# Dispatch scatters moved to other expert tiles, and a new row order for the result buffer, in an attention and mixture-of-experts kernel

## The reference

```
bids = sigmoid(einsum('bsh,eh->bse', x, conf_w) + conf_b) * wealth
top_bids, selected_experts = top_k(bids, 2)
routing_weights = softmax(top_bids, axis=-1)
expert_out = silu(x @ gate_w[e]) * (x @ up_w[e]) @ down_w[e]
x = x + sum over the two experts of routing_weight * expert_out
```

## Time and profile before

| | |
|---|---|
| median of three executions | 403.84 us |
| profiled execution | 400.13 us |
| its span, first to last instruction | 398.4 us |
| TensorE busy | 313.8 us (79%) |
| VectorE busy | 277.0 us (70%) |
| ScalarE busy | 231.0 us (58%) |
| GpSimd busy | 219.3 us (55%) |
| mean granted TensorE clock | 0.901 of full |

### The profile page before, as it was taken

How to read it: one execution, slowest core, us unless ns; L and a number is a source line. 1 busy time by engine, 2 the same in 40 slices (tenths; PEclk the granted TensorE clock), 3 DMA queues, 4 the chain that set the end, 5 groups by cost and what they waited for, 6 DMA issues and landing times.

```text
span 398.4 us, 12299 instructions
## 1 busy us (share of the span) xinstructions
PE 313.8 (79%) x4430; PEld 255.4 (64%) x4430; DVE 277.0 (70%) x770; ACT 231.0 (58%) x464; POOL 219.3 (55%) x301
## 2 busy tenths in 40 slices
PE   6797989869797977767878886779899999988400
PEld 5575756547574755557657775568788888877400
DVE  5799998797988989894745754467556556635355
ACT  4786867584775859604656834346566566646300
POOL 6202065785858688784785586545545555654300
PEclk9899988998889899865989998699999999999955
DMA  7221404114050310111322222353575574221099
GB/s 267 92 95 43 133 2 157 32 20 157 14 169 22 112 38 16 35 35 42 61 63 61 48 61 69 113 83 112 170 204 151 149 214 141 48 56 36 6 302 330
DMA packets 47722, 39.45 MB, mean 99 GB/s; under 512 B 32550, under 2 KB 39084, under 8 KB 47664
## 3 DMA queue, kind: packets, MB, share of 16 engines
q1 hardware_dynamic: 43344, 30.20, 26.5%
q0 software_dynamic: 4320, 8.47, 7.0%
HBM read 15.16 MB, written 12.21 MB: 69 GB/s over the span
## 4 chain that ended last, share of the span: by engine, by line
PE 40%; DVE 26%; ACT 11%; issue 8%; another core or an unknown queue 7%; DMA 5%; SPq 2%; DVEq 0%; ACTq 0%; POOLq 0%
PE scores L1204 6%; DVE Pm L884 5%; PE bank L1366 4%; PE bank L1364 4%; PE bank L1365 3%; PE bank L1345 3%; PE bank L1347 3%; ACT hid_hi L777 3%; DVE Kexp L1117 2%; PE bank L1346 2%; DVE Vexp L856 2%; DMA w_hi<-by_token 2%; PE scores L1347 2%; PE scores L1345 2%
## 5 line engine op out<-in xcount | busy, mean ns | idle before, releaser
L601 POOL DMA_INDIRECT by_token<-y_sb,row_meta x71 | 79.8, 1124 | 73.1 <-ACT y_sb L761 58.2
L528 POOL DMA_INDIRECT by_expert<-token_rows,rows_to x64 | 69.2, 1081 | 31.5 <-issue 17.7
L1117 DVE TENSOR_TENSOR Kexp<-hid,hid_hi 128x512 f16<-128x512 f32 x71 | 49.1, 693 | 50.4 <-ACT hid_hi L777 47.9
L1111 DVE SCALAR_TENSOR_TENSOR hid<-scores,silu 128x512 f32<-128x512 f32 x71 | 47.4, 686 | 24.2 <-remote 8.0
L1204 PE MATMUL scores<-qT,Kexp 32*128 32x128 f32 (+1 forms) x1024 | 44.0, 315 | 16.3 <-DVE Pm L884 13.7
L1204 PEld LDWEIGHTS scores<-qT,Kexp 32*128 32x128 f32 x1024 | 39.1, 221 | 26.0 <-DVE Pm L884 20.8
L777 ACT ACTIVATE hid_hi<-hid 128x512 f16<-128x512 f32 x71 | 44.6, 628 | 19.0 <-DVE hid L1111 10.5
L1364 PE MATMUL bank<-w_hi,hid_hi 128*128 x248 | 45.3, 223 | 9.3 <-DVE Kexp L1117 7.3
L770 ACT ACTIVATE silu<-bank 128x512 f32<-128x512 f32 x71 | 40.5, 597 | 20.1 <-remote 8.7
L1365 PE MATMUL bank<-w_lo,hid_hi 128*128 x248 | 44.5, 222 | 2.5 <-issue 2.4
L884 DVE TENSOR_TENSOR Pm<-scores,causal 128x512 f32<-128x512 f32 x64 | 41.1, 684 | 6.4 <-ACT Pm L683 5.3
(11 more groups left out here) (291 smaller groups left out, 741.2 us busy)
## 6 DMA issues: line engine op xcount, KB each, us to landing
w_raw<-in_w_pack_dram SPq DMA_DIRECT2D x8, 768.0 KB, 4.6
x_all<-in_x_tok_dram SPq DMA_DIRECT2D x8, 256.0 KB, 5.1
cT<-in_ctx_t_dram SPq DMA_DIRECT2D x8, 256.0 KB, 4.5
w_hi<-by_token SPq DMA_DIRECT2D x4, 512.0 KB, 7.4
w_lo<-by_token SPq DMA_DIRECT2D x4, 512.0 KB, 8.0
out_dram<-x_all SPq DMA_DIRECT2D x8, 256.0 KB, 6.3
by_expert<-pad_row SPq DMA_DIRECT2D x9, 130.0 KB
by_token<-y_sb,row_meta POOLq DMA_INDIRECT x71
```

Source lines behind the costliest of these rows:

```text
L528: pool.indirect_dma_start(by_expert, bass.IndirectOffsetOnAxis(ap=rows_to[u % 2][:, s, b:b + 1], axis=0), token_rows[u % 2][:, b, s, :], N ...
L601: pool.indirect_dma_start(by_token, bass.IndirectOffsetOnAxis(ap=row_number[:, i % METAS, s, 1:2], axis=0), y_sb[:, k, s, :], None, bounds ...
L1117: dve.tensor_tensor(hid_lo[:, k % 2, slot, :], hid[:, slot, :], hid_hi[:, k % 2, slot, :], ALU.subtract).then_inc(lo_done, 1)
```

## The change

The diff has three parts. The row order in `by_token` goes from (unit, sequence, token, choice) to (unit, token, sequence, choice): `pair_id` is made with other strides, and the view `back` that the final loads read is the matching one, so that the eight results of one partition and unit lie in 4 KB in a row. Of unit 6, piece 0 stays ahead of `tail(7)`, piece 1 comes after it, and pieces 2 and 3 follow the result scatters of tiles 0 and 1. Of unit 7, the four pieces follow the result scatters of tiles 6, 8, 9 and 11.

```diff
-            back = by_token.rearrange("(u b t s) d -> u t b s d", u=UNITS, b=UB, s=TOP)
+            back = by_token.rearrange("(u t b s) d -> u t b s d", u=UNITS, b=UB, s=TOP)
...
-            made(pool.iota(pair_id[:], [[TOP * L, UB], [1, TOP]], base=0, channel_multiplier=TOP))
+            made(pool.iota(pair_id[:], [[TOP, UB], [1, TOP]], base=0, channel_multiplier=TOP * UB))
...
             tail_rows(UNITS - 2, (UNITS - 2) % 2)
-            dispatch(UNITS - 2, range(UB - 1))
+            dispatch(UNITS - 2, [0])
             tail(UNITS - 1)
-            dispatch(UNITS - 2, range(UB - 1, UB))
+            dispatch(UNITS - 2, [1])
+
+            LAST_PIECES = (6, 8, 9, 11)
...
                                             oob_is_err=False).then_inc(y_stored[k], 16)
+                if i == 0:
+                    dispatch(UNITS - 2, [2])
+                if i == 1:
+                    dispatch(UNITS - 2, [3])
                 if i == 2:
                     tail_rows(UNITS - 1, (UNITS - 1) % 2)
                 if i == 4:
                     tail_weights(UNITS - 1, (UNITS - 1) % 2)
-                if 5 <= i < 5 + UB:
-                    dispatch(UNITS - 1, [i - 5])
+                if i in LAST_PIECES:
+                    dispatch(UNITS - 1, [LAST_PIECES.index(i)])
```

## The result

The changed kernel takes 407.83 us (median of four executions, 405.17 to 413.47) against 402.53 us (median of four, 400.96 to 405.92) for the kernel before. The ratio is 1.0166, 95% interval 1.0106 to 1.0225: slower by less than 2% but beyond the interval, where no change was forecast, and above the range of 393 to 407 us. The means of the four executions, 408.58 and 402.99 us, give 1.0139. Its profiled execution took 405.17 us, with a span of 403.4 us; before it was 400.13 and 398.4 us.

A forecast was written before the change was run, and what follows sets the result against it. It took runs of scatters to hold engines up through the expert tiles, and transfers to bound the end. -1.0 (end) - 1.6 (unit 6) + 0.9 (unit 7) = -1.7 us gave 402.1 us on the median, range 393 to 407 us.

The forecast's parts named there:

- Unit 6: Moved scatters around tail(7) and tiles 0 to 2: holes of 7.4 us against 8.96 us, gain 1.6 us (0 to 3.2).
- The sum of 22.4 us: Six long pieces of the chain between 197 and 262 us, put to no engine and no known queue.
- Runs of four or more go with the holes: GpSimd's scatters: long runs stand beside unassigned waits and pairs don't; why couldn't be read in the trace.
- Unit 7: Pieces behind tiles 6, 8, 9, 11: each still makes four scatters in a row; loss 0.9 us (0 to 1.9).
- Tile 16's load: SyncE's load after all dispatches: held 9.5 us, last scatter landing at 278.5 us, yet in time for TensorE; cost 0.
- The rival: Tile 16 late: its load comes late, TensorE stands still, later loads and copies run into each other; 409 us, chance 0.12.
- one load's cover of 0.8 us: Tile 16's load there at 283.6 us at the latest, TensorE starting at 284.40 us, so lateness costs nothing.
- The end: Closing loads read 4 KB packets in place of 1 KB: gain 1.0 us (0 to 2.0), VectorE the bound past that.
- The first sign: Closing loads: a first addition under 4.0 us after the first load's issue.
- The second: Closing loads: VectorE's 16 additions stand without a gap.
- The shrinking holes: Rival: holes shrink with distance between runs, so spreading pieces over tiles 6 to 11 gives about 392 us; chance 0.31.
- Holes that the scatters don't make: Rival: engines wait for their own code, the moves do nothing, the end alone counts; 402.8 us, chance 0.11.

The follow-up runs named there:

- f4: The changed kernel itself, run again beside the kernel before at the 365 us level: ratio 1.0185 (1.0147 to 1.0224).
- h1: The kernel before with only unit 6's pieces moved, second time, at the 400 us level: ratio 1.0171, median 403.23 us beside 399.21 us.
- the ten traces: Traces at the 400 us level, five with unit 6's move, five without: tile 0 to tile 4 takes 28.8 to 29.1 us against 21.5 to 23.4 us.
- g1: The changed kernel with the first three weight copies ahead of SyncE's wait for the dispatches, 400 us level: ratio 1.0032, median 400.53 us beside 397.15 us.
- e3: The kernel before with only unit 7's pieces moved, behind tiles 6, 8, 9 and 11, 365 us level: ratio 1.0150 (1.0104 to 1.0196).
- f1: The kernel before with unit 7's pieces behind tiles 5, 6, 7 and 11, only the last late, 365 us level: ratio 1.0159 (1.0117 to 1.0201).
- e2: The kernel before with only unit 6's pieces moved, at the 365 us level: ratio 1.0025 (0.9992 to 1.0058).
- e1: The kernel before with only the new row order, 365 us level: ratio 0.9969 (0.9933 to 1.0005), medians 363.66 and 365.70 us.
- i1: The changed kernel with the first three weight copies ahead of SyncE's wait for the dispatches, 365 us level: ratio 1.0104 (1.0053 to 1.0155).
- g3: The kernel before with the new row order and a weight copy on every second tile, 400 us level: ratio 0.9980, median 398.26 us beside 397.15 us.
- h4: The same kernel as g1, measured a second time at the 400 us level: ratio 1.0019, median 401.98 us beside 399.21 us.

## Why the prediction was wrong

**Unit 6, the step that failed.** The prediction gave this move a gain of 1.6 us. In the measured pair tile 4 came 4.1 us later (2.7 us of head start lost and more), and alone at the 400 us level the move gave 1.0171 by the ratio and 1.0099 by the means of all executions, a loss of 4 to 7 us. The working put one long run of 12 scatters at 7.4 us. Such a run came at the 365 us level (f4: 12 scatters from 191.28 to 205.67 us, and no hole). In the measured pair two runs of six came, since tile 1's results were themselves 5.42 us late and left GpSimd idle for 2.72 us. And what such runs cost was read from the chain's unassigned pieces, 15.7 us in the changed kernel. The chain counts a hole only where nothing named stands beside it: the hole of 5.42 us is not among them. The sum of 22.4 us was thus no price list. ScalarE's results tile by tile would have been. The move costs at this level by h1 and by the ten traces; its size, 0.8 to 1.7%, and why a run holds the engines up are not settled.

The rule under it was also read from too short a stretch. "Runs of four or more go with the holes" leaves out two runs of four in the same trace, from 172.2 and from 179.7 us, the dispatch of unit 5: no unassigned piece stands beside them, nor in the changed kernel or in g1. In six other traces of that level the chain holds 7.7 to 8.0 us and 5.5 us there.

**Unit 7.** At the 400 us level the term of +0.9 us (0 to 1.9) held: tiles 4 to 12 took the same time, and alone the move gave 1.0005. Each piece still stood in a row of four or six with results and still came with a hole, 3.1 to 4.0 us at ScalarE.

**Tile 16's load.** The working of its lateness was good: 280.5 us measured, 278.5 us worked out with tile 11 at its old time. Its price of nothing held in the measured pair, by the trace. The rival put 409 us on this load, close to the 407.83 us measured, but that nearness is luck: its mechanism is absent from the trace of the pair. At the 365 us level it is the whole story, as the rival had it, and with its mechanism: the queue behind the load. The working looked at one load's cover of 0.8 us. It left out that SyncE needs 4.4 us a tile from there on, which its own queue before could have told, and so never wins back what it loses. e3, f1 and f4 at 1.015 to 1.0185 show it, and e2 at 1.0025 shows that unit 6's part is small there.

**The end.** A gain of 1.0 us was forecast. The pair shows 0.4 us, and e1 alone 0.9969, which is 1.1 us of 365.7 us, with an interval that just reaches 1. The traces give the same: the mean closing stretch is 1.1 us shorter at the 365 us level and 0.4 us at the 400 us level. The first sign came true everywhere (a first addition 3.55 to 3.79 us after the first load, without the row order 3.96 to 4.15 us). The second, 16 additions without a gap, came true in e1, f4 and i1 (10.9 to 11.1 us), where VectorE is the bound as worked out, and not in the pair (12.1 us), where the last pair of loads holds them.

**The shrinking holes.** They did not come: spread over tiles 6 to 11 the pieces kept a hole each.

**Holes that the scatters don't make.** This rival is not settled. At the 365 us level 22 scatters in a row leave no hole, so scatters alone don't make them; at the 400 us level the holes move with the runs when pieces are moved, but unit 5's two runs come with and without. Against engines that wait for their code: both instruction queues move the same packets in the whole trace of the kernel before at either level (38 of 0.62 MB and 20 of 0.16 MB), and during the pieces of 2.98, 4.61, 5.80 and 3.03 us they move none.

**The size.** The parts at 400 us, by their ratios, are -0.2% (g3, which also has the copies apart) to -0.3% (e1, other level) for the row order, +1.7% for unit 6 and 0.0% for unit 7: 1.4 to 1.5%, beside 1.66% measured. By the means of all executions they are +0.1% (g3) to -0.4% (e1), +1.0% and 0.0%: 0.6 to 1.0%, beside 1.4%. The 1.6 us that the pair lost from tile 12 to tile 39 have no cause that was shown; most of it is one longer unassigned wait, and this stretch takes 97.2 to 102.2 us in the ten traces, with the move or without. At 365 us they are -0.3%, +0.25% and +1.5%: 1.45%, beside 1.85%.

## What stays open

What differs between the two levels was not found, nor why runs of scatters hold engines up at one of them, nor why unit 5's runs did so in six of ten traces. The changed kernel itself was not measured again at the 400 us level; g1 and h4, nearest to it, are at 1.0032 and 1.0019, or 1.0065 and 1.0047 by the means, and whether the three copies won something there isn't known. No run placed the scatters of one tile apart from each other in time at the 400 us level. No version beat the kernel before beyond its interval; the row order alone comes nearest (0.9969), and is the part to keep.

## What to carry to other kernels

When a late step gates a queue, compare the queue's own time for each round with the time of the work that it feeds. Here 4.4 us against 3.96 us (and against 4.3 us at the slower level) makes every microsecond of lag stay, and a cover worked out for one transfer says nothing about it. What saves the kernel then is the lead that its loads already have. Read the cost of a stall from the spacing of results on the engine that ends each round, not from the unassigned pieces of one chain. And a placement found good under one condition of the chip can be the bad one under another: the same two moves traded places between 365 us and 400 us.

## What the runs showed of the hardware

The same program on the same chip ran at 365 us and, in other measurements, at 397 us and more. At the slower level several engines stop together for 2 to 6 us (in six traces once for 7.7 to 8.0 us) beside most runs of four or more indirect DMAs of GpSimd, and single matmuls inside a product stand up to 1.2 us apart; at the faster one 22 such DMAs in a row come with none of it. The level also moves the plain pace of a tile, 3.96 us against 4.15 to 4.30 us on average. The holes cost clock too: behind the 5.42 us hole of the changed kernel the granted clock is 0.50 from 212 to 216 us, where it was 1.00 before the hole.
